# One head with both key chunks per score bank, caps of 500 columns, and squares summed by VectorE alone

## The chip, the cores and the metric

The kernel runs on one core of a Trainium2 chip. Its time is the device time of one execution in microseconds (us). Engines are named as in the profile: PE is TensorE, PEld its weight loads, DVE is VectorE, ACT is ScalarE, POOL is GpSimd, SP is SyncE, which issues most DMAs.

## The reference, cut to what matters

The program takes x of shape (32, 4, 250) through a small recurrent network (tok), an attention over 8 heads whose scores are a Gaussian of distances, and a mixture of 16 experts with two chosen per token. The change lies in the attention:

```python
xn = _ln(x, ln_scale)                       # (32, 250, 64)
Q, K, V = (einsum('bse,hef->bhsf', xn, W) for W in (W_q, W_k, W_v))
q2 = sum(Q * Q, axis=-1)[..., :, None]
k2 = sum(K * K, axis=-1)[..., None, :]
qk = einsum('bhsf,bhtf->bhst', Q, K)
sqdist = maximum(q2 + k2 - 2.0 * qk, 0.0)
scores = exp(-gamma * sqdist)
out = einsum('bhst,bhtf->bhsf', scores, V)  # no softmax
```

## The kernel before

The kernel has three stages: A, the recurrent network (up to about 105 us in the profile); B, the attention (about 105 to 545 us); C, the experts. Every engine has its own instruction list, written out by hand in order; an engine takes its list strictly in that order, and semaphores say when an instruction may start. Only the Python loops set the order, there is no scheduler.

Stage B works on 16 pairs of batch elements, one pair per step p (C = 500 columns are two batch elements of L = 250 tokens; T = 125 tokens are one key chunk, 4 chunks per pair). A step does two things at once: it prepares pair p (the "units") and it computes scores, probabilities and the product with the values for pair p-1. So steps 1 to 15 do both; step 0 only has units, and step 16 only has scores. In every engine the step is a loop over v = 0 to 7 (batch element b = v // 4, head pair v % 4), and each v has two slots:

- A **score tile** per slot, number n = 2v + c in the step. PE makes it in one of three banks (5, 6, 7) with two float32r matmuls of 500 columns (the lines in `scores`: L1058 and L1060), ACT turns it into probabilities with Exp (`exps`, L531, into one of 8 `prob` buffers), DVE caps them between two numbers per head (`caps`, L753), and PE multiplies them with the values in fp32 (`products`, L1034). A tile holds one key chunk c and two heads, 250 columns each, so a cap, whose bounds differ from head to head, is two instructions of 250 columns.
- A **unit** k = 0 to 15, spread as 0, 1, 2 in v = 1; 3, 4, 5 in v = 2; 6, 7 in v = 3; then two per v. PE makes a unit with two float32r matmuls (L1082 or, for the even ones from 8 on, L1086) in one of the banks 2, 3, 4. For k < 8 it is Q or K of one chunk, and ACT squares it (L545) into `sq[k % 2]`. Then POOL adds the two halves of each head's 64 columns (L401, into `sq2`), and DVE sums the remaining 32 per head (L763). DVE does the sum of unit k-2 where its own list comes to unit k. The even units from 8 on (`m1`, `m2`) are copied by ACT in two halves (L540) and subtracted by DVE in two halves (L769); the odd ones are values, copied by ACT (L549).

Waits: ACT's square k needs POOL's add of unit k-2, because there are two `sq` buffers; POOL's add needs DVE's sum of unit k-2, because there are two `sq2` buffers.

After the eight sums POOL multiplies them by gamma (`qkw`, L405 and L408), and only then computes the scales and the normalised tokens of the next pair (`b_scales`: L371 to L390, last the tile `xn`). PE transposes `qkw` in v = 5 (L1117) and `xn` at the start of the next step (L1015); ACT and DVE then form `s2` (L569, L794) and `s1` (L509, L513, L724).

Of the kernel before, what the change touches and what calls it, by code (L numbers as in the profile page):

```python
# [7 lines left out]
ALU = mybir.AluOpType  # L8
# [8 lines left out]
D = 64  # L17
H = 8
# [54 lines left out]
def build(nc, cst, xin, xparts, aw1, aw2, cw1, cw2, w24, wqT, wkT, wvT, woT, wq, wk, gam, lns,  # L73
          gw, gb, w1, b1, w2, b2, fg, fb, out):
    with ExitStack() as ctx:
# [56 lines left out]
        def phase(*tensors):  # L132

            with ExitStack() as scope:
                return [[scope.enter_context(nc.sbuf_tensor(f"{name}{j}", shape, dt)) for j in range(n)]
                        for name, n, shape, dt in tensors]
# [11 lines left out]
            ("wraw", 1, [128, 4, H * D], F32), ("b1m", 1, [128, G], F32), ("b2p", 1, [128, G, D], F32),  # L148
            ("awt", 1, [XK, 3, 2, D], F32), ("awr", 1, [XK, 2, 2, D], BF16))

        m1, s2, u_sb, sq, sq2, prob, y_att = phase(
            ("m1_", 2, [128, H, C], F32R), ("s2_", 2, [S_ROWS, C], F32R), ("u", 2, [T, CH, H * D], F32), ("sq", 2, [T, H, D], F32),
            ("sq2_", 2, [T, H, D // 2], F32),
            ("prob", PROBS, [T, 2, L], F32), ("y_att", 2, [128, L], F32))
        relu_sb, gated, (y_moe,), (y_low,), (yt,), (stats2,), (aggr2,), (var2,), (inv2,), (yz,), (res,), wb = phase(
            ("relu", 3, [128, C], F32), ("gated", 8, [128, C], F32), ("y_moe", 1, [128, C], F32), ("y_low", 1, [128, C], F32),
# [30 lines left out]
        def wait(eng, s, value):  # L187

            if not (isinstance(value, int) and value <= 0):
                eng.wait_ge(s, value)  # L190
# [111 lines left out]
        def _(gp):  # L302
# [90 lines left out]
            def step_b(p, j, old2, old, new, ln):  # L393
                if first_step(p):
                    b_scales(0)
                if new:
                    for k in range(8):
                        q = k % 2
                        gp.wait_ge(b_ev, 16 * p + k + 1)
                        wait(gp, b_red, 8 * p + k - 1)  # L400
                        gp.tensor_tensor(sq2[q][:, :, :], sq[q][:, :, 0:D // 2], sq[q][:, :, D // 2:D], ALU.add)\  # L401
                            .then_inc(b_sum, 1)
                    gp.wait_ge(b_red, 8 * p + 8)
                    wait(gp, b_qt, p)
                    gp.tensor_tensor(  # L405
                        qkw[:, :, Q_ROW:Q_ROW + 2 * H].rearrange("p c (a h) -> p c a h", a=2),
                        qk[:, :, 0, :].unsqueeze(2).to_broadcast([T, CH, 2, H]), gneg4, ALU.mult).then_inc(b_qkw, 1)
                    gp.tensor_tensor(  # L408
                        qkw[:, :, K_ROW:K_ROW + 2 * H].rearrange("p c (a h) -> p c a h", a=2),
                        qk[:, :, 1, :].unsqueeze(2).to_broadcast([T, CH, 2, H]), gneg4, ALU.mult).then_inc(b_qkw, 1)  # L410
                if ln:
                    b_scales(p + 1)
# [63 lines left out]
        def _(act):  # L476
# [49 lines left out]
            def step_b(p, j, old2, old, new, ln):  # L526
                def exps(v, c):
                    n = 2 * v + c
                    act.wait_ge(b_sc, 16 * (p - 1) + n + 1)
                    wait(act, b_pv, 8 * (p - 1) + v - 3)  # L530
                    act.activation(prob[n % PROBS][:, :, :], bank[5 + n % 3][0:T, 0:C].rearrange("p (h l) -> p h l", h=2),  # L531
                                   ACT.Exp).then_inc(b_exp, 1)

                def unit(k):
                    src = bank[2 + k % 3]
                    act.wait_ge(b_pj, 16 * p + k + 1)
                    if is_g(k):
                        wait(act, b_sc, 16 * (p - 1))
                        for a in range(2):
                            last = act.activation(m1[j][64 * a:64 * a + 64, k - 8 + a, :],  # L540
                                                  src[64 * a:64 * a + 64, 0:C], ACT.Copy)
                        last.then_inc(b_ev, 1)
                    elif k < 8:
                        wait(act, b_sum, 8 * p + k - 1)
                        act.activation(sq[k % 2][:, :, :], src[0:T, :].rearrange("p (h d) -> p h d", h=H), ACT.Square)\  # L545
                            .then_inc(b_ev, 1)
                    else:
                        wait(act, b_pv, 8 * (p - 1))
                        act.activation(u_sb[j][:, (k - 8) // 2, :], src[0:T, :], ACT.Copy).then_inc(b_ev, 1)  # L549

                for v in range(8):
                    if new and v == 0 and not first_step(p):
                        round_b(p, j)
                    rest = list(units(v)) if new else []
                    for c in range(2):
                        if old:
                            exps(v, c)
                        if rest:
                            unit(rest.pop(0))
                    if v == 0 and old2:  # L560
                        evac_y(p - 2, 1)
                    if v == 4 and old:
                        evac_y(p - 1, 0)
                    for k in rest:
                        unit(k)
                    if new and v == 5:
                        act.wait_ge(b_qt, p + 1)
                        wait(act, b_s2, p)
                        act.activation(rnd2[64:S_ROWS, :], bank[0][64:S_ROWS, 0:C], ACT.Copy).then_inc(b_rnd2, 1)  # L569
                    if p == PAIRS:  # L570
                        start_c(v)
# [55 lines left out]
        def _(dve):  # L627
# [116 lines left out]
                    dve.tensor_tensor(rows, part, z2[:, :, :], ALU.add).then_inc(b_res, 1)  # L744

            def step_b(p, j, old2, old, new, ln):
                def caps(v, c):
                    n = 2 * v + c
                    dve.wait_ge(b_exp, 16 * (p - 1) + n + 1)
                    for hh in range(2):  # L750
                        h = (2 * v + hh) % H
                        part = prob[n % PROBS][:, hh, :]
                        last = dve.tensor_scalar(part, part, cap_hi[0:T, h:h + 1], cap_lo[0:T, h:h + 1],  # L753
                                                 ALU.min, ALU.max)
                    last.then_inc(b_cap, 1)

                def unit(k):
                    if 2 <= k < 10:
                        n = k - 2
                        if n == 0:  # L760
                            wait(dve, b_qkw, 2 * p)
                        dve.wait_ge(b_sum, 8 * p + n + 1)
                        dve.tensor_reduce(qk[:, n // 2, n % 2, :], sq2[n % 2][:, :, :], AX.X, ALU.add)\  # L763
                            .then_inc(b_red, 1)
                    if is_g(k):
                        dve.wait_ge(b_ev, 16 * p + k + 1)
                        for a in range(2):
                            rows, h = slice(64 * a, 64 * a + 64), k - 8 + a
                            last = dve.tensor_tensor(m2[j][0:64, h, :], bank[2 + k % 3][rows, 0:C],  # L769
                                                     f32(m1[j][rows, h, :]), ALU.subtract)  # L770
                        last.then_inc(b_gl, 1)
# [161 lines left out]
        def _(pe):  # L933
# [89 lines left out]
            def products(p, v, jj, hh):  # L1023

                b = v // 4
                if hh == 0:
                    pe.wait_ge(b_cap, 16 * p + 2 * v + 2)
                    if v == 0:
                        pe.wait_ge(b_ev, 16 * (p + 1))
                    if v % 4 == 0:  # L1030
                        wait(pe, b_y, 2 * p + b)
                h = (2 * v + hh) % H
                for c in range(2):
                    last = pe.matmul(bank[1][64 * c:64 * c + 64, 0:L], u_sb[jj][:, 2 * b + c, h * D:(h + 1) * D],  # L1034
                                     prob[(2 * v + c) % PROBS][:, hh, :], start=h == 0, stop=h == H - 1)
                if hh == 1:
                    last.then_inc(b_pv, 1)

# [7 lines left out]
            def step_b(p, j, old2, old, new, ln):  # L1046
                o = 1 - j

                def scores(v, c):
                    b, hp, n = v // 4, v % 4, 2 * v + c  # L1050

                    wait(pe, b_exp, 16 * (p - 1) + (n - 2 if n > 2 else (0, -2, -1)[n]))
                    if n < 8 and c == 0:
                        pe.wait_ge(b_gl, 4 * (p - 1) + hp + 1)
                        pe.wait_ge(b_dup[hp], 32 * p)
                    cols = slice((2 * b + c) * T, (2 * b + c + 1) * T)
                    ps = bank[5 + n % 3][0:T, 0:C].rearrange("p (h l) -> p h l", h=2)
                    pe.matmul(ps, s1[o][:, cols], m1[o][:, 2 * hp:2 * hp + 2, b * L:(b + 1) * L],  # L1058
                              start=True, stop=False)
                    pe.matmul(ps, s2[o][:, cols], m2[o][:, 2 * hp:2 * hp + 2, b * L:(b + 1) * L],  # L1060
                              start=False, stop=True).then_inc(b_sc, 1)

                def unit(k):
                    dst = bank[2 + k % 3]
# [246 lines left out]
```

## Time and profile before

| | |
|---|---|
| median of 3 runs | 873.49 us (873.44 to 873.87) |
| the profiled execution | 871.59 us |
| its span, first to last instruction | 869.0 us |
| busy share of the span | PE 88%, DVE 81%, POOL 60%, ACT 57% |
| mean granted clock of PE | 0.982 |

The span is one execution as the hardware profiler recorded it; what lies around it in that execution is 871.59 - 869.0 = 2.6 us. All times inside the kernel below are from the span's start.

### The profile page before, as it was taken

How to read it: one execution, taken by the hardware profiler on the slowest of the kernel's cores; microseconds unless marked ns; L12 is line 12 of the kernel's file. 1: busy time of each engine (PE TensorE's matmuls, PEld its weight loads, DVE VectorE, ACT ScalarE, POOL GpSimd, SP SyncE). 2: the span in 40 equal slices, each digit the busy share in tenths (PEclk: the TensorE clock that was granted, in tenths of full speed). 3: DMA queues.
4: the chain of work that ended last, by engine and by line, in shares of the span. 5: the costliest groups of instructions: out<-in, count | busy, mean ns of one | idle time of the engine just before them, and what ended most of it. 6: DMA issues, size and time to landing. Idle time of an engine off the chain costs nothing.

```text
span 869.0 us, 16981 instructions
## 1 busy us (share of the span) xinstructions
PE 766.4 (88%) x5712; PEld 438.4 (50%) x5712; DVE 702.2 (81%) x1810; ACT 491.1 (57%) x913; POOL 519.9 (60%) x719
## 2 busy tenths in 40 slices
PE   1699979999999999999999999899889899998894
PEld 1234346666666666666666665344344344444341
DVE  5376768999999999999999998577787877777652
ACT  0365668877887887888788785232333333333221
POOL 7260255445445344454454452469999999999867
PEclk9999979999999999999999999899999999999997
DMA  4300021111221112211112210000000000000000
GB/s 113 136 16 2 1 49 38 36 38 38 49 50 27 39 35 50 50 41 33 38 38 50 49 33 18 1 2 7 8 7 8 7 7 14 7 8 7 8 7 18
DMA packets 22789, 25.71 MB, mean 30 GB/s; under 512 B 12816, under 2 KB 21648, under 8 KB 22576
## 3 DMA queue, kind: packets, MB, share of 16 engines
q1 hardware_dynamic: 22384, 23.85, 11.5%
q10 hardware_dynamic: 320, 0.79, 0.4%
q8 instruction: 46, 0.75, 0.4%
q14 instruction: 39, 0.32, 0.1%
HBM read 5.30 MB, written 2.43 MB: 9 GB/s over the span
## 4 chain that ended last, share of the span: by engine, by line
PE 43%; DVE 33%; POOL 11%; issue 5%; ACT 3%; DMA 2%; SPq 1%; another core or an unknown queue 1%; POOLq 0%; DVEq 0%; ACTq 0%
DVE prob L753 15%; DVE m L769 9%; PE bank L1034 6%; PE bank L962 6%; PE bank L1149 6%; PE bank L1169 6%; PE bank L1082 5%; POOL cxn L425 5%; PE bank L1058 3%; PE bank L1060 2%; DVE qk L763 2%; POOL gated L436 2%; DVE wtok L877 2%; POOL cinv L421 2%; PE bank L1160 2%
## 5 line engine op out<-in xcount | busy, mean ns | idle before, releaser
L753 DVE TENSOR_SCALAR prob<-prob,cap_hi,cap_lo 125x250 f32<-125x250 f32 x512 | 232.7, 502 | 18.6 <-ACT prob L531 15.8
L401 POOL TENSOR_TENSOR sq<-sq 125x256 f32<-125x256 f32 x128 | 96.3, 759 | 170.7 <-ACT sq L545 126.7
L884 DVE SCALAR_TENSOR_TENSOR gated<-bank,nb,wb 128x500 f32<-128x500 f32 x160 | 115.7, 732 | 71.7 <-PE bank L1149 66.4
L1169 PE MATMUL bank<-gated,w_sb 64*64 64x500 f32 x1024 | 172.8, 594 | 0.0
L1149 PE MATMUL bank<-cs,w_sb 64*64 64x500 f32 x1024 | 170.4, 587 | 0.4 <-DVE gated L884 0.4
L531 ACT ACTIVATE prob<-bank 125x500 f32<-125x500 f32 x256 | 148.6, 591 | 38.0 <-PE bank L1060 35.0
L602 ACT ACTIVATE relu<-bank,b_sb 128x500 f32<-128x500 f32 x96 | 65.0, 678 | 175.1 <-PE bank L1149 170.5
L436 POOL TENSOR_TENSOR gated<-relu,wb 128x500 f32<-128x500 f32 x96 | 125.0, 1307 | 48.0 <-ACT relu L602 48.0
L1034 PE MATMUL bank<-prob,u 125*64 125x250 f32 x1024 | 125.8, 382 | 1.5
L1058 PE MATMUL bank<-m,s 128*125 128x500 f32 x256 | 111.0, 434 | 6.1 <-issue 6.1
L1060 PE MATMUL bank<-m,s 112*125 112x500 f32 x256 | 101.0, 395 | 0.0
L1034 PEld LDWEIGHTS bank<-prob,u 125*64 125x64 f32 x1024 | 66.4, 136 | 55.3 <-issue 17.5
L769 DVE TENSOR_TENSOR m<-bank,m 64x500 fp32r<-64x500 f32 x128 | 86.3, 674 | 3.9 <-ACT m L540 1.6
L545 ACT ACTIVATE sq<-bank 125x512 f32<-125x512 f32 x128 | 76.6, 600 | 20.2 <-POOL sq L401 17.0
L1149 PEld LDWEIGHTS bank<-cs,w_sb 64*64 64x64 f32 x1024 | 54.2, 134 | 60.5 <-issue 58.4
L1082 PE MATMUL bank<-wqku_hi,s 128*125 128x512 f32 x192 | 77.7, 405 | 6.2 <-DVE m L769 3.6
L1082 PE MATMUL bank<-wqku_lo,s 128*125 128x512 f32 x192 | 76.8, 400 | 0.0
L1169 PEld LDWEIGHTS bank<-gated,w_sb 64*64 64x64 f32 x1024 | 50.7, 134 | 49.1 <-issue 46.7
L540 ACT ACTIVATE m<-bank 64x500 fp32r<-64x500 f32 x128 | 74.0, 578 | 0.8
L1058 PEld LDWEIGHTS bank<-m,s 128*125 128x125 f32 x256 | 48.0, 187 | 39.0 <-issue 32.3
L680 DVE TENSOR_SCALAR st_b<-bank 128x500 f32<-128x500 f32 x56 | 37.3, 678 | 28.2 <-PE bank L962 21.0
L962 PE MATMUL bank<-st_a,w_sb 64*64 64x500 f32 x224 | 58.7, 596 | 0.0
(165 smaller groups left out, 1371.8 us busy)
## 6 DMA issues: line engine op xcount, KB each, us to landing
m<-m SPq DMA_DIRECT2D x128, 125.0 KB, 2.3
out<-res SPq DMA_DIRECT2D x16, 125.0 KB
xa<-xparts SPq DMA_DIRECT2D x4, 281.2 KB
w_sb<-in_w SPq DMA_DIRECT2D x1, 1024.0 KB
xw<-xparts SPq DMA_DIRECT2D x4, 140.6 KB
w_sb<-in_w SPq DMA_DIRECT2D x1, 512.0 KB
m<-s SPq DMA_DIRECT2D x32, 15.6 KB
xparts<-x_part SPq DMA_DIRECT2D x1, 375.0 KB, 4.0
```

The source lines that it names most:

```text
L436: gp.tensor_tensor(gated[g % 8][:, :], relu_sb[n % 3][:, :], wb[q % 2][:, :], ALU.mult).then_inc(c_gatep, 1)
L531: act.activation(prob[n % PROBS][:, :, :], bank[5 + n % 3][0:T, 0:C].rearrange("p (h l) -> p h l", h=2), ACT.Exp).then_inc(b_exp, 1)
L753: last = dve.tensor_scalar(part, part, cap_hi[0:T, h:h + 1], cap_lo[0:T, h:h + 1], ALU.min, ALU.max)
L769: last = dve.tensor_tensor(m2[j][0:64, h, :], bank[2 + k % 3][rows, 0:C], f32(m1[j][rows, h, :]), ALU.subtract)
L884: dve.scalar_tensor_tensor(gated[g % 8][:, :], up_bank(g)[:, 0:C], nb1[:, g:g + 1], wb[q % 2][:, :], ALU.max, ALU.mult).then_inc(c_gated, 1)
L962: last = pe.matmul(dst[cols, 0:C].rearrange("p (b l) -> p b l", b=2), w24_sb[rows, 0, :], src[rows, :, 0:L], start=False, stop=True)
L1034: last = pe.matmul(bank[1][64 * c:64 * c + 64, 0:L], u_sb[jj][:, 2 * b + c, h * D:(h + 1) * D], prob[(2 * v + c) % PROBS][:, hh, :], start ...
L1058: pe.matmul(ps, s1[o][:, cols], m1[o][:, 2 * hp:2 * hp + 2, b * L:(b + 1) * L], start=True, stop=False)
L1060: pe.matmul(ps, s2[o][:, cols], m2[o][:, 2 * hp:2 * hp + 2, b * L:(b + 1) * L], start=False, stop=True).then_inc(b_sc, 1)
L1082: last = pe.matmul(dst[0:T, :], s1[j][:, c * T:(c + 1) * T], w[:, q, :], start=first, stop=not first)
L1149: last = pe.matmul(up_bank(g)[cols, 0:C], w1_sb[rows, g, cols], cs1[q % 3][rows, :], start=True, stop=True)
L1169: last = pe.matmul(y[cols, 0:C], w2_sb[rows, g, :], gated[g % 8][rows, :], start=g == 1 and rows is HI, stop=v == 7, skip_group_check=True)
```

## The change

One score tile now holds one head and both key chunks of a batch element, in the same bank and the same `prob` buffer. PE makes it with four float32r matmuls of 250 columns instead of two of 500, each with its own weight load; ACT's Exp keeps its 500 columns; the cap is one instruction of 500 columns, since both halves have the same head. The product with the values picks the other half of each buffer. Independently of that, POOL's addition of the halves is gone with its `sq2` buffers: DVE sums all 64 columns of each head straight from `sq`, and ACT's square k waits for DVE's sum of unit k-2.

```diff
@@ POOL, step_b
-                    for k in range(8):
-                        q = k % 2
-                        gp.wait_ge(b_ev, 16 * p + k + 1)
-                        wait(gp, b_red, 8 * p + k - 1)
-                        gp.tensor_tensor(sq2[q][:, :, :], sq[q][:, :, 0:D // 2], sq[q][:, :, D // 2:D], ALU.add)\
-                            .then_inc(b_sum, 1)
@@ ACT, step_b
-                                   bank[5 + n % 3][0:T, 0:C].rearrange("p (h l) -> p h l", h=2),
+                                   bank[5 + n % 3][0:T, 0:C].rearrange("p (c l) -> p c l", c=2),
...
-                        wait(act, b_sum, 8 * p + k - 1)
+                        wait(act, b_red, 8 * p + k - 1)
@@ DVE, step_b
-                    for hh in range(2):
-                        h = (2 * v + hh) % H
-                        part = prob[n % PROBS][:, hh, :]
-                        last = dve.tensor_scalar(part, part, cap_hi[0:T, h:h + 1], cap_lo[0:T, h:h + 1],
-                                                 ALU.min, ALU.max)
-                    last.then_inc(b_cap, 1)
+                    part = prob[n % PROBS][:, :, :]
+                    dve.tensor_scalar(part, part, cap_hi[0:T, h:h + 1], cap_lo[0:T, h:h + 1], ALU.min, ALU.max)\
+                        .then_inc(b_cap, 1)
...
-                        dve.wait_ge(b_sum, 8 * p + n + 1)
-                        dve.tensor_reduce(qk[:, n // 2, n % 2, :], sq2[n % 2][:, :, :], AX.X, ALU.add)\
+                        dve.wait_ge(b_ev, 16 * p + n + 1)
+                        dve.tensor_reduce(qk[:, n // 2, n % 2, :], sq[n % 2][:, :, :], AX.X, ALU.add)\
                             .then_inc(b_red, 1)
@@ PE, step_b
-                    cols = slice((2 * b + c) * T, (2 * b + c + 1) * T)
-                    ps = bank[5 + n % 3][0:T, 0:C].rearrange("p (h l) -> p h l", h=2)
-                    pe.matmul(ps, s1[o][:, cols], m1[o][:, 2 * hp:2 * hp + 2, b * L:(b + 1) * L],
-                              start=True, stop=False)
-                    pe.matmul(ps, s2[o][:, cols], m2[o][:, 2 * hp:2 * hp + 2, b * L:(b + 1) * L],
-                              start=False, stop=True).then_inc(b_sc, 1)
+                    ps = bank[5 + n % 3][0:T, 0:C].rearrange("p (c l) -> p c l", c=2)
+                    for c in range(2):
+                        cols = slice((2 * b + c) * T, (2 * b + c + 1) * T)
+                        pe.matmul(ps[:, c, :], s1[o][:, cols], m1[o][:, h, b * L:(b + 1) * L], start=True, stop=False)
+                        last = pe.matmul(ps[:, c, :], s2[o][:, cols], m2[o][:, h, b * L:(b + 1) * L],
+                                         start=False, stop=True)
+                    last.then_inc(b_sc, 1)
```

In the changed program the lines of stage B stand 7 to 9 lines higher than before (Exp L524, square L538, cap L745, sum L754, score matmuls L1051 and L1052). DVE's list in v = 2 of a step, before: `prob4` and `prob5` are the tiles of this v, the sums are those of units 1, 2 and 3.

```order
L753 TENSOR_SCALAR prob4<-prob4,cap_hi,cap_lo 125x250 [waits b_exp]
L753 TENSOR_SCALAR prob4<-prob4,cap_hi,cap_lo 125x250
L763 TENSOR_REDUCE qk<-sq2_1 125x8 [waits b_sum]
L753 TENSOR_SCALAR prob5<-prob5,cap_hi,cap_lo 125x250 [waits b_exp]
L753 TENSOR_SCALAR prob5<-prob5,cap_hi,cap_lo 125x250
L763 TENSOR_REDUCE qk<-sq2_0 125x8 [waits b_sum]
L763 TENSOR_REDUCE qk<-sq2_1 125x8 [waits b_sum]
```

The same place of DVE's list in the changed program:

```order
L745 TENSOR_SCALAR prob4<-prob4,cap_hi,cap_lo 125x500 [waits b_exp]
L754 TENSOR_REDUCE qk<-sq1 125x8 [waits b_ev]
L745 TENSOR_SCALAR prob5<-prob5,cap_hi,cap_lo 125x500 [waits b_exp]
L754 TENSOR_REDUCE qk<-sq0 125x8 [waits b_ev]
L754 TENSOR_REDUCE qk<-sq1 125x8 [waits b_ev]
```

The order is kept: each sum stands behind the cap of the slot, and the cap waits for that slot's Exp (`b_exp`). What the sum waits for is now ACT's square instead of POOL's add.

ACT's list around the same place before, from square 2 to square 5 (`prob4` and `prob5` are the Exps of v = 2):

```order
L545 ACTIVATE sq0<-bank4 125x512 [waits b_sum,b_pj]
L531 ACTIVATE prob4<-bank6 125x500 [waits b_pv,b_sc]
L545 ACTIVATE sq1<-bank2 125x512 [waits b_sum,b_pj]
L531 ACTIVATE prob5<-bank7 125x500 [waits b_pv,b_sc]
L545 ACTIVATE sq0<-bank3 125x512 [waits b_sum,b_pj]
L545 ACTIVATE sq1<-bank4 125x512 [waits b_sum,b_pj]
```

And in the changed program:

```order
L538 ACTIVATE sq0<-bank4 125x512 [waits b_red,b_pj]
L524 ACTIVATE prob4<-bank6 125x500 [waits b_pv,b_sc]
L538 ACTIVATE sq1<-bank2 125x512 [waits b_red,b_pj]
L524 ACTIVATE prob5<-bank7 125x500 [waits b_pv,b_sc]
L538 ACTIVATE sq0<-bank3 125x512 [waits b_red,b_pj]
L538 ACTIVATE sq1<-bank4 125x512 [waits b_red,b_pj]
```

Nothing moved here either; every square now waits for DVE's sum (`b_red`) of two units earlier.

PE's list at one score tile before, with the unit behind it:

```order
L1058 MATMUL bank7<-m1_0,s1_0 125x500 [waits b_dup1,b_gl,b_exp]
L1060 MATMUL bank7<-m2_0,s2_0 125x500
L1082 MATMUL bank2<-wqku_hi,s1_1 125x512 [waits b_s1,b_gl,b_ev]
L1082 MATMUL bank2<-wqku_lo,s1_1 125x512
L1058 MATMUL bank5<-m1_0,s1_0 125x500 [waits b_exp]
```

And now:

```order
L1051 MATMUL bank7<-m1_0,s1_0 125x250 [waits b_dup1,b_gl,b_exp]
L1052 MATMUL bank7<-m2_0,s2_0 125x250
L1051 MATMUL bank7<-m1_0,s1_0 125x250
L1052 MATMUL bank7<-m2_0,s2_0 125x250
L1075 MATMUL bank2<-wqku_hi,s1_1 125x512 [waits b_s1,b_gl,b_ev]
```

A tile has four matmuls of half the columns; its place among the units and its waits are as before.

## Rows read from the trace of the kernel before

**Rows 1.** The page's 40 slices of the span, busy tenths of PE and DVE.

```profile
PE 1699979999999999999999999899889899998894
DVE  5376768999999999999999998577787877777652
```

**Rows 2.** Busy time of each engine in one step of stage B, with PE's granted clock.

```profile
313.70:340.20 26.50, 25.09 (x144) 16.85 (x140) 25.25 (x63) 21.38 (x41) 12.44 (x20) 1.00 0.18 41
```

**Rows 3.** Groups of instructions over the whole span: busy us, mean ns of one.

```profile
L753 DVE TENSOR_SCALAR prob<-prob,cap_hi,cap_lo 125x250 f32<-125x250 f32 x512 | 232.7, 502 | 18.6 <-ACT prob L531 15.8
...
L401 POOL TENSOR_TENSOR sq<-sq 125x256 f32<-125x256 f32 x128 | 96.3, 759 | 170.7 <-ACT sq L545 126.7 <-DVE qk L763 34.5 <-ACT m L540 7.5
...
L763 DVE TENSOR_REDUCE qk<-sq 125x8 f32<-125x256 f32 x128 | 51.0, 407 | 3.6 <-POOL sq L401 3.5
```

**Rows 4.** ACT in order of time: start us, us (merged, xcount), idle before in brackets.

```profile
315.80 0.59 ACT L531 ACTIVATE prob<-bank 125x500 f32<-125x500 f32 x1
...
320.84 0.60 ACT L545 ACTIVATE sq<-bank 125x512 f32<-125x512 f32 x1 [0.79 <-POOL sq L401]
321.92 0.59 ACT L531 ACTIVATE prob<-bank 125x500 f32<-125x500 f32 x1 [0.48 <-PE bank L1060]
...
323.35 0.62 ACT L545 ACTIVATE sq<-bank 125x512 f32<-125x512 f32 x1
323.82 0.62 ACT L531 ACTIVATE prob<-bank 125x500 f32<-125x500 f32 x1
324.29 1.19 ACT L540 ACTIVATE m<-bank 64x500 fp32r<-64x500 f32 x2
```

**Rows 5.** DVE in order of time.

```profile
302.18 0.41 DVE L763 TENSOR_REDUCE qk<-sq 125x8 f32<-125x256 f32 x1
...
319.76 1.13 DVE L753 TENSOR_SCALAR prob<-prob,cap_hi,cap_lo 125x250 f32<-125x250 f32 x2
...
322.54 0.74 DVE L753 TENSOR_SCALAR prob<-prob,cap_hi,cap_lo 125x250 f32<-125x250 f32 x2 [0.66 <-ACT prob L531]
323.20 0.41 DVE L744 TENSOR_TENSOR h_all<-bank,z 125x256 f32<-125x256 f32 x1
...
326.64 1.35 DVE L769 TENSOR_TENSOR m<-bank,m 64x500 fp32r<-64x500 f32 x2
...
328.67 0.41 DVE L763 TENSOR_REDUCE qk<-sq 125x8 f32<-125x256 f32 x1
```

**Rows 6.** POOL in order of time.

```profile
302.66 0.42 POOL L405 TENSOR_TENSOR qkw<-qk,gneg 125x64 f32<-125x64 f32 x1 [2.92 <-DVE qk L763]
...
308.46 1.30 POOL L390 TENSOR_TENSOR xn<-z,lns_sb 125x512 f32<-125x512 f32 x1
...
319.99 0.76 POOL L401 TENSOR_TENSOR sq<-sq 125x256 f32<-125x256 f32 x1 [0.62 <-DVE qk L763]
```

**Rows 7.** PE's matmuls in order of time.

```profile
316.49 0.60 PE L1042 MATMUL bank<-c_sb,y_att 128*125 128x128 f32 x4
...
317.15 0.40 PE L1060 MATMUL bank<-m,s 112*125 112x500 f32 x1
317.39 0.40 PE L1082 MATMUL bank<-wqku_hi,s 128*125 128x512 f32 x1
...
319.32 1.91 PE L1034 MATMUL bank<-prob,u 125*64 125x250 f32 x16
```

**Rows 8.** Single lines of DVE: ns min/median/max, first and last start, forms.

```profile
L645 DVE CAST x_part<-x_res x1: 421/421/421, 8.3 to 8.3; 128x500 bf16<-128x500 f32 x1
L655 DVE CAST awr<-awt x1: 226/226/226, 17.6 to 17.6; 103x128 bf16<-103x128 f32 x1
L849 DVE TENSOR_REDUCE top<-lg x32: 204/207/219, 531.6 to 821.8; 125x4 f32<-125x64 f32 x32
```

**Rows 9.** Busy time and granted clock (the third number from the end) as stage B starts.

```profile
122.00:128.50 6.50, 3.65 (x11) 2.83 (x12) 3.27 (x6) 3.75 (x8) 3.21 (x5) 0.68 0.37 84
128.50:132.00 3.50, 3.50 (x11) 2.68 (x10) 2.94 (x13) 2.69 (x5) 0.81 (x1) 0.62 0.00 0
```

More of the change, by code:

```diff
@@ L149, in build @@
             ("awt", 1, [XK, 3, 2, D], F32), ("awr", 1, [XK, 2, 2, D], BF16))
-        m1, s2, u_sb, sq, sq2, prob, y_att = phase(
+        m1, s2, u_sb, sq, prob, y_att = phase(
             ("m1_", 2, [128, H, C], F32R), ("s2_", 2, [S_ROWS, C], F32R), ("u", 2, [T, CH, H * D], F32), ("sq", 2, [T, H, D], F32),
-            ("sq2_", 2, [T, H, D // 2], F32),
             ("prob", PROBS, [T, 2, L], F32), ("y_att", 2, [128, L], F32))
@@ L530, in exps @@
                     wait(act, b_pv, 8 * (p - 1) + v - 3)
-                    act.activation(prob[n % PROBS][:, :, :], bank[5 + n % 3][0:T, 0:C].rearrange("p (h l) -> p h l", h=2),
+                    act.activation(prob[n % PROBS][:, :, :], bank[5 + n % 3][0:T, 0:C].rearrange("p (c l) -> p c l", c=2),
                                    ACT.Exp).then_inc(b_exp, 1)
@@ L746, in step_b, with caps @@
             def step_b(p, j, old2, old, new, ln):
-                def caps(v, c):
-                    n = 2 * v + c
+                def caps(v, hh):
+                    n = 2 * v + hh
+                    h = n % H
                     dve.wait_ge(b_exp, 16 * (p - 1) + n + 1)
-                    for hh in range(2):
-                        h = (2 * v + hh) % H
-                        part = prob[n % PROBS][:, hh, :]
-                        last = dve.tensor_scalar(part, part, cap_hi[0:T, h:h + 1], cap_lo[0:T, h:h + 1],
-                                                 ALU.min, ALU.max)
-                    last.then_inc(b_cap, 1)
+                    part = prob[n % PROBS][:, :, :]
+                    dve.tensor_scalar(part, part, cap_hi[0:T, h:h + 1], cap_lo[0:T, h:h + 1], ALU.min, ALU.max)\
+                        .then_inc(b_cap, 1)
                 def unit(k):
@@ L1034, in products @@
                     last = pe.matmul(bank[1][64 * c:64 * c + 64, 0:L], u_sb[jj][:, 2 * b + c, h * D:(h + 1) * D],
-                                     prob[(2 * v + c) % PROBS][:, hh, :], start=h == 0, stop=h == H - 1)
+                                     prob[(2 * v + hh) % PROBS][:, c, :], start=h == 0, stop=h == H - 1)
                 if hh == 1:
@@ L1047, in step_b, with scores @@
                 o = 1 - j
-                def scores(v, c):
-                    b, hp, n = v // 4, v % 4, 2 * v + c
+                def scores(v, hh):
+                    b, hp, n = v // 4, v % 4, 2 * v + hh
+                    h = n % H
                     wait(pe, b_exp, 16 * (p - 1) + (n - 2 if n > 2 else (0, -2, -1)[n]))
-                    if n < 8 and c == 0:
+                    if n < 8 and hh == 0:
                         pe.wait_ge(b_gl, 4 * (p - 1) + hp + 1)
                         pe.wait_ge(b_dup[hp], 32 * p)
-                    cols = slice((2 * b + c) * T, (2 * b + c + 1) * T)
-                    ps = bank[5 + n % 3][0:T, 0:C].rearrange("p (h l) -> p h l", h=2)
-                    pe.matmul(ps, s1[o][:, cols], m1[o][:, 2 * hp:2 * hp + 2, b * L:(b + 1) * L],
-                              start=True, stop=False)
-                    pe.matmul(ps, s2[o][:, cols], m2[o][:, 2 * hp:2 * hp + 2, b * L:(b + 1) * L],
-                              start=False, stop=True).then_inc(b_sc, 1)
+                    ps = bank[5 + n % 3][0:T, 0:C].rearrange("p (c l) -> p c l", c=2)
[5 more added lines that the diff above has]
+                    last.then_inc(b_sc, 1)
                 def unit(k):
```

## The prediction

> **What bounds the kernel now.** I read the slices first: stage B, from about 105 to 545 us, is where PE and DVE are both at 9 tenths [rows 1]. The change touches nothing else. One step repeats every 26.5 us: the last sum of a step starts at 302.18 and the next step's at 328.67 [rows 5]. In that step PE is busy 25.1 us, DVE 25.3, ACT 21.4, POOL 12.4 [rows 2]. So PE and DVE are both close to full, and which one ends last has to be seen in order of time.
>
> How much does PE really need? Matmuls overlap in the record, so I count from start to start: a float32r matmul of 500 or 512 columns begins 0.24 us after the one before (317.15 to 317.39), say 0.23. A group of 8 value products takes 1.91 us, and four transposes 0.60, so 0.11 each [rows 7]. A step has 32 score matmuls and 32 unit matmuls (64 x 0.23 = 14.7), 4 groups of products (4 x 1.7 = 6.8), 12 transposes (1.3) and about 0.45 of changeover at each group: 24.6 us. PE has 1.9 us of slack per step, no more. That is the most that relieving DVE can give.
>
> The step has two parts. I cut it at the second Exp of v = 1, here e(1,1), at 315.80, and the first of v = 4, e(4,0), at 323.82 [rows 4]. The first part, 8.0 us, holds squares 2 to 7 and their sums; the other, 26.5 - 8.0 = 18.5 us, holds the m and value units and the beginning of the next step. In the first part ACT waits once for POOL's addition (0.79 us before 320.84), and for PE (0.48 before 321.92).
>
> **The change, part by part.**
>
> *Caps.* A step loses 32 caps of 250 columns and gains 16 of 500. Two caps without POOL beside them take 0.74 us, and the next instruction starts 0.66 after the first (322.54 to 323.20), so one takes 0.33 of DVE's time; with a POOL addition beside it a pair takes 1.13 [rows 5, 6]. The mean of 502 ns [rows 3] is a mixture of the two. For 250 more columns there are two slopes: a conversion in SBUF grows from 226 ns at 128 columns to 421 at 500, 0.52 ns a column, and the sum from 207 at 64 to 407 at 256, 1.04 [rows 3, 8]. The cap of 500 is thus 0.33 + 0.13 = 0.46 of DVE's time, or 0.33 + 0.26 = 0.59. I take 0.46: the conversion, like the cap, has one tensor and runs in SBUF only. The Trainium skill, SBUF — State Buffer, section on the two separate sides, says that VectorE shares a port pair with GpSimd as an exclusive lock, taken by VectorE's two-port modes and by ops with two SBUF inputs; by that rule the pair of 1.13 means that caps run in the faster mode, which is the value taken. A step saves 16 x (0.66 - 0.46) = 3.2 us of DVE, and some 8 x 0.4 = 3.2 us of stretching by the additions.
>
> *Sums.* 256 more columns at 1.04 ns: 0.41 + 0.27 = 0.67 us each, 2.1 us per step more. DVE's load falls from 25.3 to about 21 us.
>
> *Score matmuls.* 32 of 500 columns become 64 of 250, with 32 more weight loads. No row has a float32r matmul this short. The nearest: transposes with 125 loaded columns follow each other at 0.11, so a new weight load each time does not forbid that pace. Ends: 0.11 (a tile stays at 0.46) and 0.23 (half the columns save nothing, the tile takes 0.92). I take about 0.12, a tile of 0.48, because time per float32r column was the same at 500 and 512.
>
> *POOL's additions.* 128 of 0.75 us go. POOL was busy 12.4 of 26.5 us [rows 2], so nothing is gained there but the locks above and the waits.
>
> *The new wait, which decides.* Square k of ACT needed POOL's addition of unit k-2, which in turn needed DVE's sum only of unit k-4. Now it needs DVE's sum of unit k-2. In DVE's list that sum stands behind the cap of the current slot, and the cap needs the Exp that ACT has just done. So ACT and DVE now take turns. One turn, from one Exp to the next:
>
> Exp 0.59 (315.80), signal 0.03 (the Exp of 321.92 is done at 322.51, its cap starts at 322.54), cap 0.46, sum 0.67, signal 0.08 (sum done at 302.59, POOL starts at 302.66), square until the next Exp 0.47 (323.35 to 323.82): 2.30 us [rows 4 to 6].
>
> From e(1,1) to e(4,0) there are five such turns (squares 2, 3, 4, 6, 7). Square 5 follows square 4 without an Exp between, but must wait for sum 3: 0.60 more. In v = 3 the second half of the residual (0.33 until the next instruction) stands between cap and sum. Together 5 x 2.30 + 0.60 + 0.33 = 12.4 us in place of 8.0: **4.4 us lost per step**. Behind the waiting square stand ACT's next Exp, and so DVE's next cap; PE keeps going until its three score banks and three unit banks are full.
>
> *What the second part gives back.* PE arrives at it early: it no longer limits the first part, and can be done with both tiles of v = 4, their units and the products of v = 2 and 3. But the second part has a chain of its own. From e(4,0): Exp and signal 0.62, cap 0.46, sum 6 (0.60 until the next start), ACT's pair of copies (1.19) runs beside these and ends 0.1 later, DVE's pair of subtractions 1.35, cap 0.46, sum 7 0.67: 4.2 us. Then POOL: from qkw (302.66) to the end of xn (309.76) 7.1 us, during which PE's v = 5 waits for qkw as well. From there to the next e(1,1) it was 315.80 - 309.76 = 6.0 us (transposes of xn, ACT's copies, Exps, the last cap and products); shorter caps make it about 5.8. In all 4.2 + 0.1 + 7.1 + 5.8 = 17.2, where there were 18.5: **1.3 us given back** [rows 4 to 6].
>
> *Sum.* A step becomes 12.4 + 17.2 = 29.6 us, 3.1 more. Steps 1 to 15 have both halves: 15 x 3.1 = 46.5. Step 0 has squares and sums without Exps; there the pace is that of the sums instead of POOL's additions, about 1 us less. Step 16 has no squares and PE sets its pace: nothing. 871.6 of the profiled execution + 46.5 - 1 = 917.1. The median of the runs shown is 1.9 above the profiled execution: **919 us**.
>
> Its own range: if the second part runs at PE's pace with a lead of 3 us (15.4), the step is 27.8 and the time 893; if caps take 0.59 (five in the first part, four on the chain of the second: 1.2 us) and a tile 0.52 (0.5 us), the step is 31.3 and the time 945.
>
> **The rivals.**
>
> *Faster: the turns stay hidden.* DVE is relieved by 4 us and PE by nothing, so the step falls to what PE needs: 24.6 to 25.4 us, 15 x (1.1 to 1.9) = 17 to 28 us less, 845 to 856. For it speaks DVE's 25.3 of 26.5 us. It decides if a turn takes less than 8.0 / 5 = 1.6 us, or if DVE reaches the sum before the cap; the lists say that it can't, and the parts of a turn would have to lose 0.7 us. The Trainium skill's SBUF page speaks for this rival too, as its lock goes with the additions; that is priced above.
>
> *No change.* PE's lead makes good the whole loss, because the second part holds 18.5 us of which PE needs fewer: 872 to 875.
>
> *Half the columns save nothing.* At 0.23 per matmul PE needs 24.6 + 16 x 0.46 = 32 us, with some of its new waits 32 to 33: 16 x 6 = 96 us more, about 970. In the same region: PE's clock falls. While stage B started, PE was busy 3.65 of 6.5 us, and the granted clock was 0.68 and then 0.62 of full speed, means of 1.2 and 2.4 GHz [rows 9]; in the step shown it was 1.00 [rows 2]. Waits for the subtractions and for qkw will leave PE less busy; at half clock for some 4 us a step loses about 2: 950.
>
> *Short float32r matmuls run like fp32.* The 8 fp32 products of 250 columns use half of the array's columns each, two at a time, 0.42 us per two [rows 7]. A score matmul of 0.42 makes a tile 1.7 us: PE needs 24.6 + 16 x 1.2 = 44 us, 17.5 more in each of 16 steps: about 1150. Nothing in the rows shows a float32r matmul doing that.
>
> The Trainium skill, VectorE: DVE Perf Modes, the perf-mode tier table, has `tensor_reduce` at one column per cycle at most, which speaks against moving the halving to DVE; the rows of 64 and 256 columns agree, and at twice that pace a turn would be 0.27 us shorter and the time, an estimate, 24 us less.
>
> **How the numbers follow.** Turns as computed 0.60; half the columns save nothing or the clock falls 0.13; like fp32 0.10; no change 0.04; faster 0.13. A difference of 0.2% is about what a measurement of this kernel can tell from none, so slower has 0.83, the same 0.04, faster 0.13. The range of 8 in 10 is 858 to 985: it leaves out the fp32 case and most of the faster one; the likeliest case alone has 893 to 945.
>
> **What would show it.** After the change, one step should take 29 to 30 us; ACT's squares 2 to 7 should each wait for a DVE sum, 0.5 us or more, and Exps from e(1,1) to e(4,0) spread over 12 us. Caps of 500 should take 0.53 us as recorded and sums 0.67. PE should wait for score banks in the first part and for qkw in the second. I am wrong if squares start without waiting for the sums, if the matmuls of 250 columns follow each other at 0.2 us or more, or if the second part falls below 15.4 us.

## The result, and the profile after

The changed kernel takes 948.37 us (median of 4 runs, 938.74 to 950.51) where the kernel before takes 873.47 (871.88 to 873.87): a ratio of 1.085, interval 1.078 to 1.091. The prediction said 919, slower, with a range of 858 to 985. The profiled execution is the 938.74 one; its span is 936.3 us at a mean granted clock of 0.962, against 869.0 us and 0.982 before. The other timed runs have 0.950 to 0.954.

First the page's slices, as in [rows 1], and two groups of instructions, as in [rows 3]:

```profile
PE   1799888889888898898889888989898989899894
DVE  5477667766876677667776766767877787877752
...
L745 DVE TENSOR_SCALAR prob<-prob,cap_hi,cap_lo 125x500 f32<-125x500 f32 x256 | 143.6, 568 | 120.0 <-ACT prob L524 116.6
...
L538 ACT ACTIVATE sq<-bank 125x512 f32<-125x512 f32 x128 | 76.5, 599 | 95.0 <-DVE qk L754 91.8
```

DVE has fallen from 9 tenths to 6 or 7 in stage B, and PE is no longer at 9 throughout. DVE's caps are 89 us shorter in all, but DVE now idles 117 us in front of them waiting for ACT's Exp, and ACT idles 92 us in front of its squares waiting for DVE's sums. Each waits for the other. PE pays for both.

Two whole steps, the first part of one step (343.20 to 355.80), and two stretches further on in the same step (start:end, length; then busy time of PE, PEld, DVE, ACT, POOL; the third number from the end is the granted clock), as in [rows 2, 9]:

```profile
282.00:311.80 29.80, 25.67 (x174) 18.73 (x173) 21.91 (x46) 21.21 (x42) 6.44 (x12) 1.00 0.16 36
311.80:343.20 31.40, 27.15 (x175) 20.35 (x174) 21.95 (x46) 21.40 (x42) 6.36 (x12) 0.95 0.16 35
343.20:355.80 12.60, 11.34 (x77) 8.38 (x77) 7.59 (x19) 6.45 (x13) 0.00 (x0) 1.00 0.00 0
357.00:360.42 3.42, 1.70 (x9) 0.98 (x7) 3.37 (x7) 3.37 (x8) 0.14 (x1) 1.00 0.33 75
360.43:367.25 6.82, 6.09 (x24) 4.56 (x26) 5.43 (x9) 4.60 (x9) 6.12 (x12) 0.50 0.34 74
```

A step at full clock takes 29.9 us (26.5 before), although no engine is busier than 25.7 us in it. Other steps take 31.1 to 32.6: in them PE runs at half clock for a while. The last two stretches show where. PE was busy for only 1.70 of the 3.42 us up to 360.42, at a clock of 1.00; then the granted clock was 0.50 (1.2 GHz, the lower of its two levels) for 6.8 us. Taken from one second Exp of v = 1, e(1,1), to the next, the 15 steps of the profiled execution are 29.5, 29.9, 31.2, 29.9, 31.5, 29.9, 31.4, 32.6, 31.4, 31.4, 31.1, 29.9, 31.3, 32.6 and 31.3: five without a fall of the clock, ten with one or two. Their sum is 68.5 us above that of before, and the span is 67.3 us longer. So the whole loss of the profiled execution is in these steps.

ACT in order of time from e(1,1) to e(4,0) (start, us, what ended the idle time before it), as in [rows 4]:

```profile
343.37 0.59 ACT L524 ACTIVATE prob<-bank 125x500 f32<-125x500 f32 x1
...
345.23 0.60 ACT L538 ACTIVATE sq<-bank 125x512 f32<-125x512 f32 x1 [0.77 <-DVE qk L754]
345.72 0.58 ACT L524 ACTIVATE prob<-bank 125x500 f32<-125x500 f32 x1
347.56 0.60 ACT L538 ACTIVATE sq<-bank 125x512 f32<-125x512 f32 x1 [1.26 <-DVE qk L754]
348.06 0.58 ACT L524 ACTIVATE prob<-bank 125x500 f32<-125x500 f32 x1
...
353.16 0.60 ACT L538 ACTIVATE sq<-bank 125x512 f32<-125x512 f32 x1 [1.59 <-DVE qk L754]
...
356.00 0.58 ACT L524 ACTIVATE prob<-bank 125x500 f32<-125x500 f32 x1
```

And DVE beside it, as in [rows 5]:

```profile
346.34 0.54 DVE L745 TENSOR_SCALAR prob<-prob,cap_hi,cap_lo 125x500 f32<-125x500 f32 x1 [0.91 <-ACT prob L524]
346.79 0.68 DVE L754 TENSOR_REDUCE qk<-sq 125x8 f32<-125x512 f32 x1
348.68 0.54 DVE L745 TENSOR_SCALAR prob<-prob,cap_hi,cap_lo 125x500 f32<-125x500 f32 x1 [1.20 <-ACT prob L524]
```

One turn can be read off: Exp at 345.72, cap at 346.34, sum at 346.79, square at 347.56, next Exp at 348.06. That is 2.34 us, in which ACT stands still for 1.26 and DVE for 1.20. PE shows the result in v = 2, 4, 5 and 6 (as in [rows 7]):

```profile
345.43 0.28 PE L1051 MATMUL bank<-m,s 128*125 128x250 f32 x1
345.55 0.28 PE L1052 MATMUL bank<-m,s 112*125 112x250 f32 x1
345.67 0.28 PE L1051 MATMUL bank<-m,s 128*125 128x250 f32 x1
...
353.81 0.50 PE L1075 MATMUL bank<-wqku_hi,s 128*125 128x512 f32 x1 [1.13 <-ACT sq L538]
...
359.09 0.50 PE L1075 MATMUL bank<-wqku_hi,s 128*125 128x512 f32 x1 [1.12 <-DVE m L760]
...
361.16 1.08 PE L1110 MATMUL bank<-c_sb,qkw 125*112 125x125 f32 x4 [1.33 <-POOL qkw L401]
...
362.45 0.41 PE L1051 MATMUL bank<-m,s 128*125 128x250 f32 x1
362.66 0.41 PE L1052 MATMUL bank<-m,s 112*125 112x250 f32 x1
```

Score matmuls of 250 columns follow each other at 0.12 us while the clock is whole, and at 0.21 after the waits of 1.12 and 1.33 for the subtraction and for qkw. The clock fell at 360.4 us, inside the second of these waits. In the first part PE stands still twice, for 0.13 and then for 1.13 us (before 353.81), both times for a unit bank that ACT's square still holds and not for a score bank.

### The profile page after: what moved, and what is told of

It reads as the page before. It is cut to its first block, busy times and chain, and to the rows that moved or that the text cites. A ratio compares the mean times of both kernels' runs of the same rounds, so it can differ in the third digit from the quotient of the medians.

```text
span 936.3 us, 17495 instructions
## 1 busy us (share of the span) xinstructions
PE 793.7 (85%) x6224; PEld 483.8 (52%) x6224; DVE 653.1 (70%) x1554; ACT 490.4 (52%) x913; POOL 424.1 (45%) x591
## 4 chain that ended last, share of the span: by engine, by line
PE 53%; DVE 16%; POOL 12%; issue 8%; ACT 7%; DMA 2%; SPq 1%; another core or an unknown queue 0%; ACTq 0%; POOLq 0%; DVEq 0%
PE bank L1025 8%; PE bank L1075 6%; PE bank L1051 6%; PE bank L953 5%; PE bank L1142 5%; PE bank L1162 5%; DVE qk L754 5%; POOL cxn L418 5%; PE bank L1052 5%; DVE prob L745 4%; ACT prob L524 4%; DVE m L760 2%; POOL gated L429 2%; PE bank L1079 2%; DVE wtok L868 2%
## 5 line engine op out<-in xcount | busy, mean ns | idle before, releaser
L745 DVE TENSOR_SCALAR prob<-prob,cap_hi,cap_lo 125x500 f32<-125x500 f32 x256 | 143.6, 568 | 120.0 <-ACT prob L524 116.6
L398 POOL TENSOR_TENSOR qkw<-qk,gneg 125x64 f32<-125x64 f32 x16 | 8.5, 532 | 378.8 <-DVE qk L754 378.8
L524 ACT ACTIVATE prob<-bank 125x500 f32<-125x500 f32 x256 | 147.7, 588 | 35.7 <-PE bank L1052 33.9
L1051 PE MATMUL bank<-m,s 128*125 128x250 f32 x512 | 147.2, 310 | 8.3 <-issue 8.3
L1052 PE MATMUL bank<-m,s 112*125 112x250 f32 x512 | 136.7, 290 | 0.0
L538 ACT ACTIVATE sq<-bank 125x512 f32<-125x512 f32 x128 | 76.5, 599 | 95.0 <-DVE qk L754 91.8
L1051 PEld LDWEIGHTS bank<-m,s 128*125 128x125 f32 x512 | 101.1, 197 | 40.1 <-issue 29.2
L1075 PE MATMUL bank<-wqku_hi,s 128*125 128x512 f32 x192 | 83.2, 433 | 41.5 <-DVE m L760 19.8
L1052 PEld LDWEIGHTS bank<-m,s 112*125 112x125 f32 x512 | 101.4, 198 | 5.7
L760 DVE TENSOR_TENSOR m<-bank,m 64x500 fp32r<-64x500 f32 x128 | 86.5, 675 | 18.6 <-ACT m L533 17.3
L1025 PEld LDWEIGHTS bank<-prob,u 125*64 125x64 f32 x1024 | 68.5, 139 | 47.3 <-issue 13.9
L754 DVE TENSOR_REDUCE qk<-sq 125x8 f32<-125x512 f32 x128 | 85.4, 678 | 1.3 <-ACT sq L538 1.0
```

The costliest lines, as they stand in the source:

```text
L754: dve.tensor_reduce(qk[:, n // 2, n % 2, :], sq[n % 2][:, :, :], AX.X, ALU.add)\
L1051: pe.matmul(ps[:, c, :], s1[o][:, cols], m1[o][:, h, b * L:(b + 1) * L], start=True, stop=False)
L1052: last = pe.matmul(ps[:, c, :], s2[o][:, cols], m2[o][:, h, b * L:(b + 1) * L], start=False, stop=True)
L1075: last = pe.matmul(dst[0:T, :], s1[j][:, c * T:(c + 1) * T], w[:, q, :], start=first, stop=not first)
```

## The experiments

All were timed in three rounds beside the kernel before, which had 873.45 us in the first four and 872.84 in the last four. Theory throughout: the loss comes from ACT and DVE taking turns, because a square waits for a sum that stands behind the cap of the Exp just made, and PE's gaps then cost a second time through the clock. The rivals: the longer sums cost DVE's time; the four short matmuls cost PE's; the clock alone is to blame.

**The two halves of the change.** First the scores and caps of the new form, with POOL's additions back:

```diff
...
+                        gp.tensor_tensor(sq2[q][:, :, :], sq[q][:, :, 0:D // 2], sq[q][:, :, D // 2:D], ALU.add)\
+                            .then_inc(b_sum, 1)
...
-                        wait(act, b_red, 8 * p + k - 1)
+                        wait(act, b_sum, 8 * p + k - 1)
...
-                        dve.tensor_reduce(qk[:, n // 2, n % 2, :], sq[n % 2][:, :, :], AX.X, ALU.add)\
+                        dve.tensor_reduce(qk[:, n // 2, n % 2, :], sq2[n % 2][:, :, :], AX.X, ALU.add)\
```

> Only the score part of the change: one head and both chunks per tile, one cap of 500 columns, score matmuls of 250 columns; POOL adds the halves of the squares as before. My theory (the squares' wait for DVE's sum behind the cap makes ACT and DVE take turns) expects no turns here: squares 2 to 7 pass in about 8 us, a step falls from 26.5 to 25.0-26.0 us, 848 to 866 us in all, clock as before. The rival (the 250-column matmuls or the new tiles cost the time) expects most of the loss here: 910 us or more.

Measured: 854.85 us, 0.977 (0.973 to 0.982). Steps are 25.3 us and the first part 8.1. Its groups of caps and sums, and ACT in the first part:

```profile
L752 DVE TENSOR_SCALAR prob<-prob,cap_hi,cap_lo 125x500 f32<-125x500 f32 x256 | 155.7, 619 | 60.2 <-ACT prob L531 56.0
...
L761 DVE TENSOR_REDUCE qk<-sq 125x8 f32<-125x256 f32 x128 | 51.3, 409 | 4.0 <-POOL sq L401 3.8 <-issue 0.2
```

```profile
332.98 0.60 ACT L531 ACTIVATE prob<-bank 125x500 f32<-125x500 f32 x1
...
337.26 0.60 ACT L545 ACTIVATE sq<-bank 125x512 f32<-125x512 f32 x1 [0.41 <-POOL sq L401]
...
341.07 0.62 ACT L531 ACTIVATE prob<-bank 125x500 f32<-125x500 f32 x1
```

So the new scores and caps are worth 18.6 us by themselves; the short matmuls cost nothing that shows. Then the other half: scores and caps as before, squares summed by DVE alone (of the edit, against the changed kernel, the caps).

```diff
...
-                    part = prob[n % PROBS][:, :, :]
-                    dve.tensor_scalar(part, part, cap_hi[0:T, h:h + 1], cap_lo[0:T, h:h + 1], ALU.min, ALU.max)\
-                        .then_inc(b_cap, 1)
+                    for hh in range(2):
+                        h = (2 * v + hh) % H
+                        part = prob[n % PROBS][:, hh, :]
+                        last = dve.tensor_scalar(part, part, cap_hi[0:T, h:h + 1], cap_lo[0:T, h:h + 1],
+                                                 ALU.min, ALU.max)
+                    last.then_inc(b_cap, 1)
...
```

> Only the squares part: DVE sums 64 columns per head straight from ACT's squares and ACT's square k waits for the sum of unit k-2; tiles and caps of 250 columns as before. My theory: a turn has two caps of 0.33 in place of one of 0.46, so 2.5 us; the stretch from the second Exp of v = 1 to the first of v = 4 takes 13.4 us, a step 30.5 without a fall of the clock, and with falls 31 to 32.5: 932 to 962 us in all. The rival (matmuls or tiles) expects about 873 us.

Measured: 966.48 us, 1.105 (1.101 to 1.109), a little above what was expected; the first part is 13.6 us, since a turn now holds two caps, and steps take 31.0 to 33.9 (those without a fall of the clock 31.0 to 31.3, where 30.5 was expected). Its groups of caps and sums, and the waits between 300 and 380 us (total us, times, longest):

```profile
L746 DVE TENSOR_SCALAR prob<-prob,cap_hi,cap_lo 125x250 f32<-125x250 f32 x512 | 196.3, 430 | 104.2 <-ACT prob L524 101.6
...
L756 DVE TENSOR_REDUCE qk<-sq 125x8 f32<-125x512 f32 x128 | 85.4, 679 | 1.3 <-ACT sq L538 1.2
```

```profile
ACT sq L538 <- DVE qk L756: 18.9, 13, 1.8
DVE prob L746 <- ACT prob L524: 17.0, 19, 1.6
```

The halves add up: -18.6 and +93.0 make +74.4, and the whole change makes +74.9. The loss is all in the squares. That the sum fits to 0.5 us is partly chance: alone, the new caps and scores bring the step down to what PE needs, while beside the new wait they shorten a turn.

**The wait or the sum.** Four `sq` buffers in place of two, so that square k needs the sum of unit k-4; all else as in the changed kernel.

```diff
-("sq", 2, [T, H, D], F32)
+("sq", 4, [T, H, D], F32)
...
-                        wait(act, b_red, 8 * p + k - 1)
+                        wait(act, b_red, 8 * p + k - 3)
```

> The changed kernel with four square buffers in place of two, so that square k waits for the sum of unit k-4. Nothing else differs. My theory: the turns are gone, PE sets the pace again, a step takes 25 to 26 us: 848 to 866 us, and the clock stays at full speed in the attention. The rival (the longer sums or the longer chain to the transposes of qkw cost the time, not the wait for the buffer) expects 900 us or more.

Measured: 862.43 us, 0.986 (0.982 to 0.989); steps 25.8. Its squares and what they waited for, then ACT in the first part:

```profile
L538 ACT ACTIVATE sq<-bank 125x512 f32<-125x512 f32 x128 | 73.8, 611 | 2.8 <-PE bank L1075 2.4 <-DVE qk L754 0.3
...
335.70 0.60 ACT L524 ACTIVATE prob<-bank 125x500 f32<-125x500 f32 x1
336.16 1.11 ACT L538 ACTIVATE sq<-bank 125x512 f32<-125x512 f32 x2
337.52 0.59 ACT L524 ACTIVATE prob<-bank 125x500 f32<-125x500 f32 x1 [0.25 <-PE bank L1052]
...
341.88 0.59 ACT L524 ACTIVATE prob<-bank 125x500 f32<-125x500 f32 x1 [1.83 <-PE bank L1052]
...
343.79 0.62 ACT L524 ACTIVATE prob<-bank 125x500 f32<-125x500 f32 x1
```

The sums are as long as before the edit (679 ns), and still 86 us are gone: the squares' waits for DVE have fallen from 91.8 us to 0.3 in the whole span, ACT waits for PE instead, the first part is 8.1 us, and the clock keeps 1.00 from 131 to 539 us. DVE's longer sum is not the loss; the wait is. With three buffers (square k needs the sum of k-3):

```diff
+("sq", 3, [T, H, D], F32)
...
+                        wait(act, b_red, 8 * p + (k - 2 if k > 2 else min(k - 1, 0)))
```

> The changed kernel with three square buffers: square k waits for the sum of unit k-3, which stands behind the cap of the slot before. By my theory one slot of slack is enough, because a turn then spreads over two slots: a step of 25.8 us as with four buffers, 856 to 870 us. If the slack has to be two slots, the time lies between: 880 to 920 us.

Measured: 866.11 us, 0.993 (0.991 to 0.995); steps 26.1, first part 8.8. The third buffer brings 82 us, the fourth 4. Now two buffers again, with only DVE's list changed: the sum of a slot stands ahead of its cap.

```diff
...
+                        if rest:
+                            sums(rest[0])
...
                         caps(v, c)
...
-                            unit(rest.pop(0))
+                            unit(rest.pop(0), first=False)
```

> The changed kernel with one swap in DVE's list: in each slot the sum of unit k-2 stands ahead of the slot's cap, not behind it. Still two square buffers. My theory says that the loss comes from the sum standing behind a cap that waits for ACT's newest Exp; then the swap alone takes the turns away, squares 2 to 7 pass in 8 to 9 us and a step takes 25.5 to 26.5 us: 856 to 874 us. If two buffers are too few whatever the order (the rival), the time stays at 920 us or more.

Measured: 863.64 us, 0.989 (0.986 to 0.991). ACT in the first part:

```profile
336.27 0.60 ACT L524 ACTIVATE prob<-bank 125x500 f32<-125x500 f32 x1
...
338.13 0.60 ACT L538 ACTIVATE sq<-bank 125x512 f32<-125x512 f32 x1 [0.78 <-DVE qk L754]
...
340.47 0.60 ACT L538 ACTIVATE sq<-bank 125x512 f32<-125x512 f32 x1 [0.29 <-DVE qk L754]
...
345.11 0.58 ACT L524 ACTIVATE prob<-bank 125x500 f32<-125x500 f32 x1
```

Squares still wait for sums here, but no longer for a sum that waits for the newest Exp. Of squares 2 to 7 two do not wait, the waits of the others shrink to between 0.29 and 0.78, and the first part is 8.8 us. This tells the turns apart from "ACT waits for DVE" as such. Both edits together:

> The changed kernel with four square buffers and the sum ahead of the cap, as a candidate for the best version. With four buffers a step was 25.8 us, 0.5 more than with the scores part alone (25.3), and PE waited for qkw, which needs the last sum. If the later last sum is that 0.5, the swap gives it back: a step of 25.2 to 25.5 us, 850 to 857 us. If not, 858 to 864 us.

Measured: 854.50 us, 0.979 (0.977 to 0.980); steps 25.3. One stretch of 30 us of it, and then one of the kernel with POOL's additions:

```profile
280.00:310.00 30.00, 29.65 (x202) 22.61 (x202) 25.95 (x58) 25.48 (x51) 7.11 (x12) 1.00 0.17 37
```

```profile
280.00:310.00 30.00, 29.43 (x205) 22.78 (x202) 23.59 (x60) 24.71 (x49) 14.11 (x23) 1.00 0.16 37
```

PE is busy 29.4 to 29.7 of 30 us in both, whether DVE has 26 or 24 us and POOL 7 or 14. Without the turns PE is the bound, and taking POOL out of the squares brings no further time. These two beat the kernel before by 2.1 and 2.3%, and don't differ measurably.

**The length of the sum inside a turn.** DVE sums 32 of each head's 64 columns; the other half of the sum of squares is left out.

```diff
-                        dve.tensor_reduce(qk[:, n // 2, n % 2, :], sq[n % 2][:, :, :], AX.X, ALU.add)\
+                        dve.tensor_reduce(qk[:, n // 2, n % 2, :], sq[n % 2][:, :, 0:D // 2], AX.X, ALU.add)\
```

> The changed kernel, but DVE sums only the first 32 of each head's 64 squares (half of the sum is left out, so the distances are not the reference's). A turn then loses 0.27 us. My theory: the stretch of squares 2 to 7 falls from 12.6 by 6 x 0.27 = 1.6 to 11.0 us, a step without a fall of the clock from 29.9 to 28.0, and the time to 893 to 922 us, depending on how often the clock falls. If the wait for the buffer is not the cause, the shorter sum saves at most what DVE lacks, which is nothing: 938 us or more.

Measured: 908.95 us, 1.041 (1.040 to 1.043); the first part is 11.2 us. DVE's sum in one turn, and that turn of ACT from Exp to Exp:

```profile
335.06 0.41 DVE L754 TENSOR_REDUCE qk<-sq 125x8 f32<-125x256 f32 x1
...
333.99 0.58 ACT L524 ACTIVATE prob<-bank 125x500 f32<-125x500 f32 x1
335.57 0.60 ACT L538 ACTIVATE sq<-bank 125x512 f32<-125x512 f32 x1 [1.00 <-PE bank L1075]
336.06 0.58 ACT L524 ACTIVATE prob<-bank 125x500 f32<-125x500 f32 x1
```

The turn is 2.07 us, 0.27 less than 2.34, as long as the sum is shorter (412 ns against 679). The steps without a fall take 28.2 us, so 15 x 1.7 = 25 of the 39 us come from the turns. The rest fits with fewer falls of the clock: eight spells of half clock in these steps by its profile, twelve in the changed kernel's. Even with the sum of before, the kernel with turns is 36 us slower than the kernel before. (The row puts the wait at 335.57 down to PE, because a unit's matmul ended about then. That was unit 5. Square 3 needs unit 3, whose last matmul started at 333.74 already, and DVE's sum of unit 1, which ended at 335.47: it waited for the sum.)

**The clock.** PE gets nine matmuls in v = 5, four behind the scores and five ahead of the wait for qkw. They write into a bank that nobody reads then; no other work changes.

```diff
...
+                def filler(n):
+                    wait(pe, b_res, p - 1)
+                    for _ in range(n):
+                        pe.matmul(bank[0][0:T, :], s1[j][:, 0:T], wqku_hi[:, 0, :], start=True, stop=True)
...
+                        if old and new and v == 5 and c == 1:
+                            filler(4)
...
+                        if old:
+                            filler(5)
```

> The changed kernel with nine more matmuls per step on PE, whose results nobody reads, in the two waits of v = 5 (four before unit 11, five before the transposes of qkw). If the fall of the granted clock behind these waits is what makes some steps 31.3 to 32.6 us long and others 29.9, then the clock stays at full speed in the attention and all steps take 29.9 to 30.2: 920 to 928 us. If the clock is only a sign of something else, the time stays at 938 us or more.

Measured: 920.88 us (920.08 to 926.37), 1.055 (1.050 to 1.060). Stretches of 30 us of stage B:

```profile
252.00:282.00 30.00, 27.71 (x182) 20.38 (x181) 21.77 (x46) 21.26 (x41) 6.43 (x12) 1.00 0.16 36
...
312.00:342.00 30.00, 27.94 (x184) 20.38 (x183) 22.04 (x47) 21.26 (x41) 6.43 (x12) 1.00 0.16 36
342.00:372.00 30.00, 27.91 (x184) 20.46 (x185) 22.03 (x46) 21.26 (x41) 6.43 (x12) 1.00 0.16 37
```

The clock stays at 1.00, the steps take 29.9 us (29.5 to 30.2), and the first part is still 12.6. More work on PE makes the kernel 27.5 us faster; in the two profiled executions the fifteen steps are 16.8 us shorter. So of the 74.9 us, 27.5 are the clock, and 47.4 are what is left at full clock: the turns, less what the new caps give back. The rival that the clock alone is to blame falls.

## Why the prediction was right, and where its size was not

**The new wait: right.** A turn was predicted at 2.30 us and is 2.34; the first part at 12.4 and is 12.6; the second at 17.2 and is 29.9 - 12.6 = 17.3 where the clock doesn't fall; the step at 29.6 and is 29.9. Of its signs, two are not as written: square 5 follows square 4 at once, so that five of the six squares wait (0.77 to 1.59 us), and PE waits in the first part for a unit bank, not for score banks. Four buffers or the swap of sum and cap remove the turns, and with them the loss.

**Operations: right.** Caps of 500 take 0.54 us (median) as recorded, predicted 0.53, and the next instruction starts 0.45 behind them, predicted 0.46. Sums take 0.68 (0.67); 256 columns more cost 679 - 412 = 267 ns, 1.04 ns a column, against the run with half the columns. Matmuls of 250 columns take 0.12 each (0.12), which ends the rivals "half the columns save nothing" and "like fp32". The Trainium skill, VectorE: DVE Perf Modes, the perf-mode tier table, has `tensor_reduce` in the 1x mode only, one column per cycle, and a cycle of the 0.96 GHz in that page's specifications is 1.04 ns; the trace agrees.

**The sum: one term missing.** The step of the prediction that failed is the one that put the clock among the rivals, under "half the columns save nothing" ("at half clock for some 4 us a step loses about 2: 950"), and gave the forecast no term for it. The forecast's own sum holds for a kernel whose clock doesn't fall: 919 predicted, 920.9 measured with the filler. But the prediction itself named the waits for the subtraction and for qkw; they are the ones of 1.12 and 1.33 us between which PE has two matmuls to do, and the fall came in ten of fifteen steps of the profiled execution, 1.2 to 2.7 us each. [Rows 9] had shown such a fall at the start of stage B. With the 27.5 us that the filler took away, 1.8 a step, the forecast would have been 946. So the time lies 3 us above the likeliest case's own range of 893 to 945, inside the range as a whole, and at the 950 of that sub-case, which had some 4 us a step at half clock; the profiled execution has 41 us in fifteen steps, 2.7 a step.

The median stands 9.6 us above the profiled execution, where it had been 1.9. The clock explains most of that by an estimate: from 0.962 to 0.952 is 2% of the span more at half clock, 19 us, between five and six falls of 3.4 us at about 1.5 each, 8 us. No timed run's trace shows where they fell.

**The faster rival: right price, wrong kernel.** It gave 845 to 856 if the turns stay hidden, and two kernels that hide them have 854.5 and 854.9, with steps of 25.3 us where PE's need had been counted at 24.6 to 25.4. Its second condition, that DVE reaches the sum before the cap, was what the swapped order made true; that alone gave 863.6, above this rival's range, because with two buffers some squares still wait (a first part of 8.8 us). The 854.5 needed four buffers as well.

**Stretching by POOL: right, and worth little.** Caps of 250 have a mean of 430 ns without the additions, 502 with them [rows 3]; caps of 500 have 619 with them and 568 without. The prediction's pair "without POOL beside them" (322.54) was not quite that, since an addition is recorded until 322.81; but with no additions at all, in the run of the squares alone, one cap starts 0.33 after the other just as there. The Trainium skill, SBUF — State Buffer, section on the two separate sides, has VectorE and GpSimd share a port pair as an exclusive lock; the trace agrees that caps beside POOL are longer. But the kernel with the stretched caps is as fast as the best one without, since DVE is not the bound there.

## What to carry to other kernels

When a change replaces a buffer's wait, look in the releasing engine's list for what stands ahead of the release. If that needs the waiting engine's newest output, the two engines take turns, however little busy they are, and one buffer more or a swap of two instructions was worth 82 to 85 us here. Then follow the gaps to PE and give them a second term in the sum, because where PE had waited the clock fell as well, and that was 27 of 75 us.

## What the runs showed of the hardware that was not expected

- PE lost its clock around waits of 1.1 to 1.4 us each, two in a step (v = 5), in ten of fifteen steps; the other five have the same waits and kept it. In the step shown it was busy 1.70 of the 3.42 us before the fall, and then had 0.50 for 6.8 us, although it was busy 6.09 of them. With half the sum, waits of 0.83 to 1.11 us were enough in eight of fifteen steps. The same steps with nine matmuls that nobody reads keep 1.00, and so did the kernel before, whose steps have one wait of up to 1.00 us for qkw.
- Float32r matmuls of 250 columns with a new weight load of 125 columns each follow each other at 0.12 us, half of the 0.23 to 0.24 for 500 columns [rows 7].
